# Causal mask of two attentions moved from TensorE to VectorE, one head loop written out

## The reference, cut to what matters

```
# layer 2: q and k rotated, 4 key heads, each shared by 4 query heads
s = einsum('bghid,bgjd->bghij', q * D**-.25, k * D**-.25)
s = s - 1e30 * (i < j)                 # causal
p = softmax(s);  o = p @ v;  r = o @ w_ao
# layer 3: 16 key heads
scores = einsum('biph,biqh->biqp', k, q)
attn = softmax((scores * mask - 1e10 * (1 - mask)) / sqrt(128))
z = attn @ v;  out = W_O @ z
```

## Time and profile before

| | |
|---|---|
| median of 3 runs | 1489.52 us (1486.38 to 1491.92) |
| profiled execution | 1481.4 us, span 1479.6 us |
| PE busy | 1340.7 us, 91% |
| DVE busy | 724.0 us, 49% |
| ACT busy | 622.4 us, 42% |
| third attention | about 597 to 882 us |
| fourth attention | about 994 to 1359 us |

### The profile page before, as it was taken

One profiled execution on the slowest core, in us unless ns is written; L12 is line 12 of the kernel. 1 busy time (PEld: TensorE's weight loads), 2 busy tenths in 40 slices (PEclk: granted clock), 3 DMA queues, 4 the chain that ended last, 5 costly groups with the idle time before them and its releaser, 6 DMA issues.

```text
span 1479.6 us, 20970 instructions
## 1 busy us (share of the span) xinstructions
PE 1340.7 (91%) x6796; PEld 820.1 (55%) x6802; DVE 724.0 (49%) x1713; ACT 622.4 (42%) x1516; POOL 68.0 (5%) x79
## 2 busy tenths in 40 slices
PE   5888888768999997999999999979999999999995
PEld 3633443462243736555656558756666666666863
DVE  4676535451223232787887762134433343345547
ACT  2534443279931110354555540335444444443043
POOL 2410000150000000000000000000000000000000
PEclk9998999858999999899999999999999999999998
DMA  5000000300010001000000000110000000000000
GB/s 142 1 2 1 1 18 1 147 1 1 1 68 0 0 0 69 21 12 12 12 11 8 11 1 0 68 60 22 18 14 21 11 21 21 11 21 0 1 1 28
DMA packets 17566, 31.85 MB, mean 22 GB/s; under 512 B 3049, under 2 KB 15177, under 8 KB 16356
## 3 DMA queue, kind: packets, MB, share of 16 engines
q1 hardware_dynamic: 17076, 28.94, 5.8%
q0 software_dynamic: 432, 2.16, 0.8%
HBM read 32.11 MB, written 1.05 MB: 22 GB/s over the span
## 4 chain that ended last, share of the span: by engine, by line
PE 73%; DVE 13%; issue 8%; ACT 4%; POOL 1%; SPq 0%; DMA 0%; DVEq 0%; POOLq 0%; ACTq 0%
PE bank L730 12%; PE bank L913 9%; PE bank L747 8%; PE bank L737 7%; PE bank L723 5%; PE bank L715 5%; PE bank L742 4%; PE bank L933 4%; PE bank L634 4%; PE bank L618 3%; PE bank L535 2%; DVE W L1435 1%; PE bank L965 1%; PE bank L589 1%; PE bank L951 1%
## 5 line engine op out<-in xcount | busy, mean ns | idle before, releaser
L989 ACT COPY R<-bank 128x512 f32<-128x512 f32 (+4 forms) x180 | 106.0, 610 | 319.1 <-PE bank L747 152.1
L1504 DVE TENSOR_REDUCE nm<-bank 128x1 f32<-128x128 f32 (+3 forms) x256 | 124.6, 488 | 183.7 <-PE bank L738 183.5
L730 PE MATMUL bank<-XNT,W 128*128 128x512 f32 x416 | 203.9, 615 | 3.8 <-ACT R L989 2.5
L1122 ACT ACTIVATE R<-bank,nm 128x128 f32<-128x128 f32 (+3 forms) x256 | 136.1, 532 | 101.6 <-DVE nm L1504 100.6
L737 PE MATMUL bank<-R 128*128 128x512 f32 (+3 forms) x384 | 135.0, 435 | 0.0
L1097 ACT ACTIVATE PT<-bank 128x512 f32<-128x512 f32 (+3 forms) x256 | 109.3, 522 | 46.3 <-PE bank L623 41.6
L715 PE MATMUL bank<-W,R 128*128 128x256 f32 x576 | 125.3, 380 | 1.8 <-ACT R L989 1.8
L913 PE MATMUL bank<-XNT,W 128*128 (+2 forms) x256 | 120.4, 614 | 1.4 <-DVE R L1614 1.3
L730 PEld LDWEIGHTS bank<-XNT,W 128*128 128x128 f32 x416 | 71.9, 192 | 86.6 <-issue 66.2
L715 PEld LDWEIGHTS bank<-W,R 128*128 128x128 f32 x576 | 109.1, 190 | 17.2 <-issue 1.9
L742 PE MATMUL bank<-identf,R 128*128 128x128 f32 x640 | 112.6, 275 | 5.2 <-DVE R L1521 3.6
(11 more groups left out here) (206 smaller groups left out, 1836.2 us busy)
## 6 DMA issues: line engine op xcount, KB each, us to landing
W<-in_wq SPq DMA_DIRECT2D x32, 128.0 KB, 2.0
W<-in_wo SPq DMA_DIRECT2D x2, 2048.0 KB, 8.7
W<-in_wk SPq DMA_DIRECT2D x20, 128.0 KB, 2.1
W<-in_wv SPq DMA_DIRECT2D x20, 128.0 KB, 2.0
W<-in_wa SPq DMA_DIRECT2D x2, 1024.0 KB, 5.1
W<-in_wb SPq DMA_DIRECT2D x2, 1024.0 KB, 7.1
W<-in_ed SPq DMA_DIRECT2D x1, 1792.0 KB, 14.5
W<-in_eg SPq DMA_DIRECT2D x1, 1760.0 KB, 6.9
```

What stands on the lines that cost most here:

```text
L730: ins = mm(bank[:, :], wqkv23[:, s, c, :], XNT[:, c, b * SEQ:(b + 1) * SEQ], start=c == 0, stop=c == DC - 1)
L989: return nc.scalar.copy(dst, src)
L1122: return fn(Pr[c][:, 0:n], PS[c][:, 0:n], ACT.Exp, bias=nm[:, c:c + 1], accum_out=esum[:, c:c + 1])
L1504: return dve.tensor_reduce(nm[:, u % 4:u % 4 + 1], PS[u % 4][:, 0:(u % TPB + 1) * P], AX.X, ALU.max, negate=True)
```

## The change

`score_tile` loses its mask matmul: the score matmul stands alone. `max_tile` becomes one `tensor_tensor_reduce` over the tile: it adds a row of the mask (zeros, and -1e30 above the diagonal of the last 128 columns) to the scores, multiplies by -1, writes the result back to the same bank in PSUM and keeps the row minimum, starting from 1e30, in `nm`. So the bank holds negated scores, and `exp_tile` takes scale -1. The mask row is a new table `mask_row` of 128 x 512 bf16. It lies in the space of `sel1`, now part of `seltab` of 128 partitions, and is loaded by SP after the second feed-forward part; DVE waits for five loads instead of four (80 instead of 64). In `attention3` the loop over heads becomes a Python loop on PE, ACT and DVE; SP keeps its loop. The layers before are as they were.

```diff
--- before.py
+++ after.py
@@ -78,7 +78,9 @@
         mask_qk = sb("mask_qk", [P, P], BF16)
         mask_kq = sb("mask_kq", [P, P], BF16)
 
-        sel1 = sb("sel1", [3 * E + 3, E * IE + HS1], BF16)
+        seltab = sb("seltab", [P, E * IE + HS1], BF16)
+        sel1 = seltab[0:3 * E + 3, :]
+        mask_row = seltab[:, 0:SEQ]
         rope1 = sb("rope1", [P, 2, TPB, HD])
         rw0 = sb("rw0", [P, DC, E])
         rw1 = sb("rw1", [P, DC, E + 1])
@@ -330,6 +332,7 @@
             sp.dma_start(wo23, W["wo2"]).then_inc(ld["wo2"], 16)
             sp.wait_ge(ffn[1]["y_ps"], NT)
             sp.dma_start(rope2, W["rope2"]).then_inc(ld["ffn2"], 16)
+            sp.dma_start(mask_row, W["mask_row"]).then_inc(ld["ffn2"], 16)
             sp.dma_start(wa, W["wa2"]).then_inc(ld["ffn2"], 16)
             sp.dma_start(wb, W["wb2"]).then_inc(ld["ffn2"], 16)
             sp.dma_start(bout, W["bout2"]).then_inc(ld["ffn2"], 16)
@@ -734,8 +737,7 @@
             def score_tile(u, q, k):
                 t = u % TPB
                 n = (t + 1) * P
-                mm(PS[u % 4][:, 0:n], q[:, t * P:n], k[:, 0:n], start=True, stop=False)
-                return mm(PS[u % 4][:, t * P:n], identb[:, :], mask_qk[:, :], start=False, stop=True)
+                return mm(PS[u % 4][:, 0:n], q[:, t * P:n], k[:, 0:n], start=True, stop=True)
 
             def turn_tile(u):
                 for j in range(u % TPB + 1):
@@ -879,7 +881,7 @@
                     if b == 0:
                         for u in range(4):
                             scores(0, u, need[0])
-                with pe.Fori(0, NH - 1) as i:
+                for i in range(NH - 1):
                     body(i, False)
                 body(NH - 1, True)
 
@@ -1119,7 +1121,7 @@
 
             def exp_tile(u):
                 c, n = u % 4, (u % TPB + 1) * P
-                return fn(Pr[c][:, 0:n], PS[c][:, 0:n], ACT.Exp, bias=nm[:, c:c + 1], accum_out=esum[:, c:c + 1])
+                return fn(Pr[c][:, 0:n], PS[c][:, 0:n], ACT.Exp, scale=-1.0, bias=nm[:, c:c + 1], accum_out=esum[:, c:c + 1])
 
             def copy_pt(u, slot):
                 t = u % TPB
@@ -1223,7 +1225,7 @@
                         for u in range(3):
                             exponent(0, u)
                 body(0, True, False)
-                with act.Fori(1, NH - 1) as i:
+                for i in range(1, NH - 1):
                     body(i, False, False)
                 body(NH - 1, False, True)
                 store_output(NH - 1, B - 1, NH * B - 1)
@@ -1501,12 +1503,15 @@
                 body(NG - 1, True)
 
             def max_tile(u):
-                return dve.tensor_reduce(nm[:, u % 4:u % 4 + 1], PS[u % 4][:, 0:(u % TPB + 1) * P], AX.X, ALU.max,
-                                         negate=True)
+
+                n, s = (u % TPB + 1) * P, PS[u % 4]
+                return dve.tensor_tensor_reduce(out=s[:, 0:n], in0=s[:, 0:n], in1=mask_row[:, SEQ - n:SEQ], scale=-1.0,
+                                                scalar=-MASKED, op0=ALU.add, op1=ALU.min,
+                                                accum_out=nm[:, u % 4:u % 4 + 1])
 
             def attention2():
                 ca = corea[0]
-                dve.wait_ge(ld["ffn2"], 64)
+                dve.wait_ge(ld["ffn2"], 80)
 
                 def maximum(u):
                     dve.wait_ge(ca["s_ps"], u + 1)
@@ -1588,7 +1593,7 @@
                             maximum(0, u)
                 normalise(0, 0)
                 normalise(0, 1)
-                with dve.Fori(0, NH - 1) as i:
+                for i in range(NH - 1):
                     body(i, False)
                 body(NH - 1, True)
 
@@ -1780,6 +1785,7 @@
     t = {"identf": np.eye(P, dtype=np.float32), "identb": np.eye(P).astype(bf)}
     later = np.triu(np.ones((P, P)), 1) * MASKED
     t["mask_qk"] = later.astype(bf)
+    t["mask_row"] = np.concatenate([np.zeros((P, SEQ - P)), later], 1).astype(bf)
     t["mask_kq"] = np.ascontiguousarray(later.T).astype(bf)
     owner = np.arange(E * IE) // IE
     one = (owner[None] == np.arange(E)[:, None]).astype(np.float32)
```

## The result

The changed kernel took 1473.92 us in the median (1471.32 to 1478.69), the kernel before, run beside it, 1483.59 (1480.92 to 1491.92). The ratio is 0.9928, 95% interval 0.9909 to 0.9946: a gain of 10.7 us, between 8.0 and 13.5. Forecast were 13.7 us and 1475.8. The profiled execution took 1471.32 us, span 1469.5, against the 1479.6 of before.

A forecast was written before the change was run, and what follows sets the result against it. TensorE, busy for 91% of the span, was taken as the bound. Savings of 6.0 us in the third attention and 7.7 in the fourth made 13.7, taken off a median of 1489.5: 1475.8 us, range 1466 to 1484.

The forecast's parts named there:

- Mask, 0.055 and 0.05 behind it: TensorE, both attentions: each removed mask matmul saves 0.055 us, a projection behind one 0.05 more, unless a wait absorbs it.
- Rival C: Masks save only 0.055 us each, new instruction holds VectorE and delays its result by 0.20; gain 7.1, 1482.4; chance 0.13.
- A: Rival: all 256 masks, 0.05 at 137 places behind them and 1.0 for loops regained; 22.0 us, 1467.5; chance 0.08.
- Plain units: Third attention, ten units without k or v projection: rotation loop loses two masks and 0.05, 0.16 us each, 1.6 in all.
- New instruction: VectorE's add, negate, write back and minimum: main part costs what the maximum did, result 0.02 us later, VectorE held 0.08 longer.
- rival B: VectorE runs the new instruction at half rate, 1.33 us more a unit; gain 8.3, 1481.2; chance 0.12.
- k units: Third attention, six units with a k projection: 0.16 us each saved, less 0.1 in all for the later maximum.
- Units after k: Third attention, six units following those with a k projection: no wait, 0.27 us each, 1.6 in all saved.
- v units: Third attention, six units with a v projection: no wait, two projections, 0.32 us each, 1.9 in all saved.
- The three last units: End of the third attention, units without projection: give back about the 0.3 us added by the first four maxima.
- Fourth attention: Two waits a head absorb three masks; 0.475 us a head saved, 7.1 over 15 heads, 7.7 with start and last head.
- rival D: Fourth attention's written-out heads stall TensorE for code, 2.0 us a head, 30 us: 16 slower, 1505.8; chance 0.07.

The follow-up runs named there:

- scale_before_rotation: Kernel after, with VectorE making the third tile's scaled row ahead of the q rotation in the third attention; 1470.2 us, ratio to before 0.9909.
- copy_before_exponent: Kernel after, with ScalarE copying the second tile's transposition ahead of the next unit's first exponent in the third attention; 1469.3 us, ratio to before 0.9911.
- copy_before_output: both_orders plus ScalarE copying the first tile's transposition ahead of the last unit's output in the third attention; 1462.1 us, ratio to before 0.9844.
- both_masks: Kernel after with the mask matmuls back beside the new instruction; 1485.2 us, ratio to before 1.0010.
- no_mask_old_maximum: Kernel after with the old maximum and exponent, so the causal mask is left out altogether; 1467.8 us, ratio to before 0.9911.
- mask_twice: Kernel before with each mask matmul issued twice; 1490.9 us, ratio to before 1.0041.
- loops_kept: Kernel after with the fourth attention's loops back on TensorE and ScalarE, VectorE still written out; 1474.4 us, ratio to before 0.9941.
- orders_with_masks: Kernel before with heads written out and the two order changes of both_orders, keeping mask matmuls and old maximum; 1477.5 us, ratio to before 0.9943.
- both_orders: Kernel after with the scaled row ahead of the rotation (third attention) and v copied ahead of the output (fourth); 1456.5 us, ratio to before 0.9830.

## Why the prediction was right or wrong

**The time.** 1475.8 was forecast, 1473.9 measured, inside 1466 to 1484, faster as forecast. The level is nearer than the gain deserves: I took the gain off a median of three runs, 1489.5, and more runs of the kernel before gave 1483.6. The gain was too large by 3 us: 13.7 is just outside the measured 8.0 to 13.5. That 1475.8 came within 2 us of the measured time is in part luck, since the two errors cancel.

**Mask, 0.055 and 0.05 behind it.** Both right. Doubling the mask gave 0.052 to 0.058 for each; the projection fell from 1.77 to 1.72. Rival C (no 0.05, and 0.20 for the new instruction) and A (all regained) fall.

**Plain units, 1.6 us forecast, 0.7 measured.** The first of the steps that failed. The loop over the rotation was right, as scale_before_rotation shows (7.76 to 7.27), the two masks outside it saved nothing, as said, and once the copy is out of the way (copy_before_exponent) the unit has the forecast length to 0.01 us. But "it holds two of the four masks" took all of TensorE's stretch in the loop for its own work. With one mask gone, the stretch between the third and the fourth transposes waits for ScalarE's copy, which hangs on the new maximum. Piece by piece, before against after: third to fourth transposes 1.09 and 1.12, from there to the projection 1.36 and 1.32, the projection to the rotation's start 1.97 and 1.92, and from there to the third transposes 3.40 both times. That sums to 7.82 and 7.76.

**New instruction.** The main part was right to 0.01 us at 512, and rival B (half rate) is out. The accumulator read is there, but took 142 ns and not the 81 of the earlier trace rows. The size of the delay was wrong: 0.02 forecast, 0.07 measured. "In a plain unit hidden" was a statement on VectorE's idle time, while the cost came by the exponent. VectorE, held 0.01 us longer for each, does hide that. One reading was wrong too. The row of L1717 gives the type of its first source only; the second is `tern`, which the kernel has as bf16 (L172). So it is no row of two f32 sources, and the prediction's sentence that it contradicts the rule cited there does not stand: no run here has the accumulating form with two f32 sources in SBUF. The cost taken from the row stands, as an f32 and a bf16 source are what the new instruction has.

**k units, 0.14 forecast, 0.10 measured**: 0.17 for the masks and the projection (0.16), less 0.07 for the later result (0.02). **Units after k, 0.27 forecast, 0.18 measured**: "no wait" was true of before alone. TensorE had ended its second score tile just as ScalarE's copy freed the bank. Without the first two masks it gets there 0.11 us earlier and waits 0.11, so these two save nothing. copy_before_output gives it back. **v units, 0.32 forecast, 0.35 measured**: right.

**The three last units** I expected to be 0.3 us shorter, and they are 0.12 longer; both_masks is 0.18 longer there and no_mask_old_maximum 0.05 shorter. So the new instruction costs 0.17 there; that it does so by its late result is likely, but not shown. **The first four maxima**, back to back behind the last rotation, I had at 0.3. In the kernel before and then in the kernel after, up to the reciprocal that follows them:

```profile
611.54 1.68 DVE L1504 TENSOR_REDUCE nm<-bank 128x1 f32<-128x128 f32 x4
613.13 0.15 DVE L1518 RECIPROCAL erec<-esum 128x1 f32<-128x1 f32 x1
```

```profile
608.61 0.29 DVE L1508 CUSTOM_DVE_ANT_0 bank<-bank,seltab 128x128 f32<-128x128 f32 x1
...
610.36 0.16 DVE L1523 RECIPROCAL erec<-esum 128x1 f32<-128x1 f32 x1
```

That is 1.59 and 1.75 us, so each holds VectorE 0.04 longer when another one follows it, and the first transposes come 0.17 later, in all the kernels with the new instruction. The two terms, plus 0.3 and minus 0.3, were to cancel; they are plus 0.17 and plus 0.12. The distance from the start of the third attention to its first value product (25.05 us before, 25.09 after) looks as if nothing was lost, but it cannot be compared: the granted clock differed, before and then after,

```profile
594.00:600.00 6.00, 5.33 (x14) 3.15 (x13) 0.26 (x1) 1.86 (x4) 0.00 (x0) 0.50 0.01 3
```

```profile
594.00:600.00 6.00, 5.32 (x17) 2.70 (x16) 2.27 (x4) 1.22 (x3) 0.00 (x0) 0.96 0.02 7
```

and from 612 to 618 us it was 1.00 before and 0.75 after. In mask_twice, with neither of the two low stretches, the same distance is 23.31 us.

**Fourth attention, 0.475 a head forecast, 0.45 measured**, 22.17 for 22.15. Right, and the two waits that absorb three masks are confirmed: with the one at the q projection removed the masks' worth rose from 0.46 to 0.64. Both waits grew: the one at the q projection from 0.17 to 0.27 recorded (0.11 forecast), the one for v by 0.06 in the loop, as forecast, and by 0.15 written out.

**Heads written out, 0 forecast.** 0.01 us a head dearer in the kernel before, 0.05 in the kernel after, 0.8 us in all: the wrong side of the 0 to 1.0 saved, and far from rival D's 30 us, which is out. The heads repeat to 0.01 us, though more code was moved: the instruction queue carried 0.54 MB in loops_kept, and after (packets, MB, share of the queues, from the page of the profile):

```profile
q8 instruction: 45, 0.74, 0.2%
```

**The mask row's load.** The bias behind it landed 9.8 us after its issue, where it took 7.9 before: 1.9 us for the "few tenths" of the prediction. The cover held. It landed at 595.1 us and the first rotation began at 597.7, when TensorE's first projection had ended. These 2.6 us are 4.3 less than before: 1.8 because that projection was shorter at the higher granted clock, the rest because the loads landed later.

**Slips in the rivals.** The stall of 0.9 us a head in D is where the gain is used up (13.7 over 15), not where slower can be told from no change; the "third rival" named as the bound for written-out heads is D, the fourth; and the 0.12 in C for units after k is not derived. None of them moves the forecast.

## What to carry to other kernels

Where no wait stands in the trace, removing work saves only up to the next date of another engine: look for the resource that will be reached next (here a bank that ScalarE empties), and compare the distance from that copy's start to what follows it in several units. Price a new instruction twice, by how long it holds its engine and by when its result can be used. Before two stretches are compared, look whether the granted clock was the same in both. Two orders of steps (a scaled row behind a rotation, a copy of the output ahead of the copy that frees a bank) held 13 us, more than 256 matmuls; with both changed the kernel takes 1.7% less than before, where the masks alone gave 0.7%.

## What was not expected of the hardware

The stretch from the last value product of the third attention to the first of the fourth holds a feed-forward part, whose code is the same, and the fourth's first projections. It took 134.5 us before, 134.5 with both masks, 136.7 written out with masks, 137.2 in orders_with_masks, 133.9 in copy_before_exponent, and 136.4 after: it does not go with the change. TensorE's first eight projection matmuls there, before:

```profile
994.30 3.70 PE L730 MATMUL bank<-XNT,W 128*128 128x512 f32 x8 [0.68 <-ACT XNT L989]
```

and after:

```profile
988.92 6.16 PE L733 MATMUL bank<-XNT,W 128*128 128x512 f32 x8 [0.68 <-ACT XNT L991]
```

The table of the stretch around them, after (granted clock third from the end):

```profile
988.00:993.00 5.00, 4.33 (x7) 1.83 (x6) 0.00 (x0) 0.86 (x3) 0.00 (x0) 0.50 0.00 0
993.00:998.00 5.00, 5.00 (x27) 3.48 (x26) 1.50 (x5) 1.42 (x3) 0.00 (x0) 0.91 0.00 0
```

TensorE had been nearly idle for some microseconds before both (busy for 0.03 us from 985 to 990 before, for 0.43 from 980 to 985 after), and the granted clock had fallen to 0.50, the 1.2 GHz level. Before, it was back at 1.00 when the eight matmuls began (0.95 over 993 to 998); after, it rose within them, which made them 2.5 us dearer. That is a quarter of what this change is worth, and in the profiled execution it went against it. At the start of the third attention each of the two kernels lost some 1.7 us in the same way, at different places. The first 600 us, the same in all kernels, differ too: the granted clock from 100 to 200 us was 0.91 in the kernel before and 0.97 in both_orders, whose first value product came 2.7 us earlier. And the end of the program, from the last value product on, took 123.4 us in the profiled executions of eight of these kernels and 125.1 in five, whatever the change. I did not follow this further.

The engine named for a weight load's wait need not be the one that ended it: the record named VectorE (0.50 us) where moving a copy of ScalarE took all but 0.23 of the wait away. And recorded idle time of TensorE was 0.27 us where the wait cost 0.43.
